# Six transfers with rows of 2 KB in place of two with rows of 8 and 4 KB for each expert's weights

## The reference, cut to what matters

```python
TOPK, E, h, i = 2, 16, 512, 256
probs = jax.nn.softmax(xt @ Wr.T + bias, axis=-1)
topk_val, topk_idx = jax.lax.top_k(probs, TOPK)
w = topk_val / (jnp.sum(topk_val, axis=-1, keepdims=True) + EPS)
g = jnp.einsum('th,ehi->tei', xt, Wg)
u = jnp.einsum('th,ehi->tei', xt, Wu)
y = jnp.einsum('tei,eih->teh', jax.nn.silu(g) * u, Wd)
routed = jnp.einsum('tke,tk,teh->th', one_hot(topk_idx), w, y)
shared = (jax.nn.silu(xt @ sWg) * (xt @ sWu)) @ sWd
```

## Time and profile before

| | |
|---|---|
| median of 3 runs | 1112.99 us (1108.66 to 1118.93) |
| the profiled execution | 1113.7 us, of which the span from the first to the last instruction is 1111.8 us |
| mean granted TensorE clock | 0.964 of full speed |
| PE busy over the span | 1005.3 us (90%) |
| POOL busy over the span | 298.5 us (27%) |
| DMA, mean over the span | 103 GB/s, 44573 packets |
| q1 (SyncE's), q0 (GpSimd's) | 26.7% and 11.9% of the 16 engines' span |

### The profile page before, as it was taken

One profiled execution on the slowest core, in us unless ns is written; L12 is line 12 of the kernel. 1 busy time (PEld: TensorE's weight loads), 2 busy tenths in 40 slices (PEclk: granted clock), 3 DMA queues, 4 the chain that ended last, 5 costly groups with the idle time before them and its releaser, 6 DMA issues.

```text
span 1111.8 us, 22306 instructions
## 1 busy us (share of the span) xinstructions
PE 1005.3 (90%) x6879; PEld 643.5 (58%) x6880; DVE 551.8 (50%) x1422; ACT 499.1 (45%) x1195; POOL 298.5 (27%) x319
## 2 busy tenths in 40 slices
PE   6767699999989999899998899899998999899994
PEld 3323458576765857567585687778643444344442
DVE  7985347465645756365666677678511111111110
ACT  7512277676747777576768622211122222122221
POOL 1087220111102010020202036342223443344442
PEclk9889899999989999899999999999999999999998
DMA  5032733240513324041335111611288447944443
GB/s 200 29 86 83 180 77 81 67 112 6 135 45 77 78 57 98 32 110 45 78 78 192 41 75 58 244 69 48 78 253 237 89 89 198 290 87 85 94 85 47
DMA packets 44573, 114.37 MB, mean 103 GB/s; under 512 B 9332, under 2 KB 11380, under 8 KB 42162
## 3 DMA queue, kind: packets, MB, share of 16 engines
q1 hardware_dynamic: 32146, 87.14, 26.7%
q0 software_dynamic: 12320, 25.90, 11.9%
HBM read 53.03 MB, written 25.17 MB: 70 GB/s over the span
## 4 chain that ended last, share of the span: by engine, by line
PE 67%; DMA 9%; DVE 8%; issue 8%; POOL 4%; ACT 2%; POOLq 0%; ACTq 0%; DVEq 0%
PE psum L512 10%; PE psum L1241 10%; PE psum L478 7%; DMA out<-y_sb,slot_out 7%; PE psum L525 7%; PE psum L499 7%; PE psum L483 5%; PE psum L1320 5%; PE psum L1185 4%; PE psum L1169 3%; PE psum L1262 2%; PE psum L528 1%; PE psum L501 1%; PE psum L1284 1%; DMA x_rows<-xn_scratch,slot_tok 1%
## 5 line engine op out<-in xcount | busy, mean ns | idle before, releaser
L635 DVE TENSOR_REDUCE nmax<-psum 128x1 f32<-128x128 f32 (+7 forms) x256 | 192.3, 754 | 79.4 <-PE psum L501 72.2
L594 ACT ACTIVATE probs<-psum,nmax 128x128 f32<-128x128 f32 (+7 forms) x256 | 190.7, 745 | 51.0 <-DVE nmax L635 45.7
L1241 PE MATMUL psum<-attnT,x_T 128*128 x376 | 180.9, 604 | 4.2 <-issue 2.4
L512 PE MATMUL psum<-ident,probs 128*128 128x128 f32 x1152 | 176.1, 279 | 3.9 <-DVE probsT L581 1.5
L499 PE MATMUL psum<-k_stack,q_stack 128*128 128x512 f32 (+2 forms) x384 | 158.2, 466 | 22.5 <-issue 14.3
L579 ACT COPY probsT<-psum 128x512 f32<-128x512 f32 (+3 forms) x256 | 129.1, 504 | 57.4 <-PE psum L512 45.6
L1142 DVE COPY x_T<-psum 128x512 f32<-128x512 f32 x47 | 32.5, 692 | 240.5 <-PE psum L1284 240.5
L478 PE MATMUL psum<-xnT,w_unit 128*128 128x512 f32 x256 | 132.6, 608 | 0.2 <-ACT full L453 0.2
L512 PEld LDWEIGHTS psum<-ident,probs 128*128 128x128 f32 x1152 | 125.6, 143 | 9.1 <-DVE probsT L581 3.8
L425 POOL CAST part_hi<-full 128x512 fp32r<-128x512 f32 x32 | 19.6, 612 | 376.6 <-ACT full L453 268.7
L842 POOL DMA_INDIRECT out<-y_sb,slot_out x47 | 74.5, 1586 | 166.5 <-DMA out<-y_sb,slot_out 74.3
(11 more groups left out here) (220 smaller groups left out, 1440.4 us busy)
## 6 DMA issues: line engine op xcount, KB each, us to landing
attnT<-in_wgu SPq DMA_DIRECT2D x16, 1024.0 KB, 5.2
q_stack<-part_hi SPq DMA_DIRECT2D x64, 128.0 KB, 2.4
q_stack<-part_lo SPq DMA_DIRECT2D x64, 128.0 KB, 2.4
k_stack<-part_hi SPq DMA_DIRECT2D x64, 128.0 KB, 2.4
k_stack<-part_lo SPq DMA_DIRECT2D x64, 128.0 KB, 2.6
w_dn<-in_wd SPq DMA_DIRECT2D x16, 512.0 KB, 6.1
out<-acc SPq DMA_DIRECT2D x17, 256.0 KB, 2.0
hot_all<-xn SPq DMA_DIRECT2D x4, 1024.0 KB, 8.5
```

Of the source, the lines that this page charges most:

```text
L512: mm = pe.transpose(bank(4 + m % 2)[:, (j - 4 * k) * P:(j - 4 * k + 1) * P], probs[n % PSLOTS][:, j * P:(j + 1) * P], ident[:, :])
L594: act.activation(probs[n % PSLOTS][:, 0:(i + 1) * P], bank(2 * (n % 2), 2)[:, 0:(i + 1) * P], ACT.Exp, bias=nmax[:, n % 4:n % 4 + 1], scal ...
L635: dve.tensor_reduce(nmax[:, n % 4:n % 4 + 1], bank(2 * (n % 2), 2)[:, 0:(i + 1) * P], AX.X, ALU.min).then_inc(s_M, 1)
L1241: mm = pe.matmul(bank(2 + p), lhs(k), rhs(k), start=(k == 0), stop=(k == KC - 1), skip_group_check=True)
```

## The change

`load` issues an expert's weights as six transfers instead of two, one for each block of 128 along the contraction: four of 128 x 512 values for gate and up, two of 128 x 512 for down. Each transfer is 256 KB with one row of 2 KB for each partition. Before, gate and up were one transfer of 1 MB whose partition rows are 8 KB, and down one of 512 KB with rows of 4 KB. In HBM the rows of one such transfer now lie 8 KB apart (gate and up) and 4 KB apart (down), since the layout of the arrays is unchanged. The number that `ready` waits for follows (six times 16 for each round of the ring instead of two times 16). The bytes moved, the slots, the places in the program and all other waits are the same.

```diff
             def load(e, s):
-                src_gu = a["wgu"][bass.ds(e, 1), :, :, :].rearrange("o p k n -> (o p) k n")
-                src_dn = a["wd"][bass.ds(e, 1), :, :, :].rearrange("o p k n -> (o p) k n")
-                sp.dma_start(w_gu[:, s, :, :], src_gu).then_inc(s_wl[s], 16)
-                sp.dma_start(w_dn[:, s, :, :], src_dn).then_inc(s_wl[s], 16)
+                for k in range(KC):
+                    sp.dma_start(w_gu[:, s, k, :], a["wgu"][bass.ds(e, 1), :, k, :].rearrange("o p n -> (o p) n")
+                                 ).then_inc(s_wl[s], 16)
+                for k in range(2):
+                    sp.dma_start(w_dn[:, s, k, :], a["wd"][bass.ds(e, 1), :, k, :].rearrange("o p n -> (o p) n")
+                                 ).then_inc(s_wl[s], 16)
 
             def ready(m, s):
 
-                sp.wait_ge(s_wl[s], 32 * (m + 1))
+                sp.wait_ge(s_wl[s], 16 * (KC + 2) * (m + 1))
                 sp.sem_inc(s_wr, 1)
```

## The result

The changed kernel takes **1134.1 us** (median of 4 runs, 1131.6 to 1137.6) against 1113.0 before (1108.7 to 1118.9): a ratio of 1.0188, with a 95% interval of 1.0134 to 1.0242. That is 21 us slower. The forecast was 1116 us with a range of 1105 to 1127, so the time lies outside it. The profiled execution took 1131.6 us with a span of 1129.6, 17.8 more than the span of before.

A forecast was written before the change was run, and what follows sets the result against it. The prediction took SyncE's load-loop period to bound the two routed stretches. Twelve loads at +0.25 us each gave +3.0 us, with issue, completion, HBM gaps and the first four loads at nothing: 1116 us, range 1105 to 1127.

The forecast's parts named there:

- the period of the load loop is what the stretches are made of: Routed stage, loads of experts 4 to 9 and 10 to 15: SyncE's load period of 7.64 and 7.75 us holds the adds.
- +0.24 us a load: DMA engines: an expert's 1.573 MB in 2 KB rows takes 3.93 us instead of 3.69; 0.25 taken.
- the issue costs nothing: SyncE's six issues, 0.54 us apart, stay hidden behind the load's bytes, with 0.9 us of cover.
- completion ... is in the 0.25: Six semaphore posts per load instead of two add nothing beyond the 0.25 us for bytes; upper bound +1.2 a load.
- rival B: Routed stretches: adds take turns with loads, load period grows to 10.5 us; about +11 us, 1124 us; chance 0.15.
- The fixed 2.0 us for each transfer: Skill's cost beside the bytes: four more transfers would add 8 us a load if paid serially; the prediction set it aside.
- Rival D: Weight loads: strided or small reads run slower, +1.2 us a load, 14.4 us over twelve loads, 1127 us; chance 0.13.
- C: Routed stretches: adds get in and loads hardly pay; at most -11.5 us, 1101.5 us, likelier 1107; chance 0.17.
- E: Weight loads: no effect, since 8 KB rows are cut up on the way anyway; 1113 us; shares 0.55 with the forecast.

The follow-up runs named there:

- six transfers by partitions: Against the changed kernel, the six 256 KB transfers are cut by partitions (four of 32, two of 64) with 8 and 4 KB rows; 1145.6 us, ratio 1.0290.

## Why the prediction was wrong

**The bound was read one step too far.** The step "the period of the load loop is what the stretches are made of" does not hold for the kernel before: freeing SyncE there gained nothing. With adds and gathers left out TensorE ran through the first stretch without a wait, at a load period of 7.30 us. The prediction's own sum pointed there: it had expert 15 ready 4.9 us before TensorE began its tiles. The step does hold for the changed kernel in its second stretch, where the chain is the load loop's, and freeing SyncE gives back 17 us in all. The row that I took for proof, six waits for landings against one for TensorE, shows that SyncE was busy waiting, not that anyone waited for it.

**The cost of a load was mis-sized more than tenfold.** The step "+0.24 us a load" was measured at 2.9 (7.70 to 10.60 in the mean of both stretches). The experiments part it:
- 0.5 us for 2 KB rows, with the number of transfers unchanged and the engines to themselves. The forecast had 0.25 for bytes through full engines; that was half in size, and only about 0.1 of the 0.5 is longer work of the engines.
- 0.9 us for six transfers, with their gaps in HBM. Here "the issue costs nothing" was right (0.52 us each, as forecast), and "completion ... is in the 0.25" failed. The stretch of twelve back-to-back 256 KB transfers at 395 to 405 GB/s was no stand-in: it reads without gaps and its transfers stood in a queue that was already deep, while a load of the ring begins on idle engines and moves 271 to 365 GB/s in its middle. Which of the two differences counts was not tried apart.
- 1.5 us beside adds and gathers: 8.58 to 10.60 is 2.0, where the kernel before pays 0.5. Two transfers with small rows pay 1.9 of the same kind (7.70 to 9.63), so small rows are enough for it. They are not the only way: six transfers by partitions pay 1.4 with large rows (10.25 to 11.63). So more, smaller transfers and smaller rows each make a load slower beside GpSimd's transfers, and the two don't add up. That the engines take up the adds sooner when the pieces are smaller fits the landings of the adds, but how they share their time was not traced.

**What that part is, was rival B.** Its mechanism came out: adds pass loads (0.8 and 4.7 us before their load's landing), and the load pays. Its sizes came out too, but in part by luck: a period of 10.5 us was worked out, 10.84 and 10.36 measured, and the second stretch was to cost 11.8 us more and cost 11.0. B put 2.95 us on a load, 0.25 for its own bytes and 2.7 for the adds and gathers let in. Measured were 1.4 and 1.5, an error on each side, and the two cancel. I gave it 0.15, because nothing in the rows showed an add overtaking a load. That was the wrong question. Loads in the routed stage of the kernel before came in large pieces only, so its rows could not show what small ones do. B's reckoning missed on one side: in the first stretch it had a gain of 1 us, and 5.6 were lost. Adds there also landed late (6.6 us in the median, up to 8.3), as did gathers, and TensorE waited 8.3 us for rows. The premise that the add lands after 5.3 us failed; the add can pass a load but doesn't run undisturbed.

The Trainium skill's rule (page "DMA: Bandwidth & Descriptors", section "Queues, rings and completion order"), by which the engines take turns between queues a packet at a time, agrees with adds that pass loads now. No run here shows how large a packet in this sense is (the packets that the profile counts are single rows): two transfers in small rows and six in large rows both grow beside adds. The fixed 2.0 us for each transfer that the prediction takes from the same page is given there for transfers that GpSimd issues; four more transfers of SyncE cost 0.9 us here, not 8.

**Rival D** named strided or small reads as slow, +1.2 us each load. The load did grow by 1.4 us with the engines to itself, so D's size was near. Its cause was not: without the gaps 14 of the 21 us remain, clear of noise, and of the 1.4 us the small rows account for 0.5. D had no term for adds that pass.

**Rivals C and E** fell: nothing was gained, the rows of 8 KB went as single packets, and small rows do something by themselves.

**The clock** was in no term. In the timeline of PE in the changed kernel, the first gate and up behind the 5.5 us wait for weights takes 3.78 us, and one behind a short wait 1.98. A down step of two tiles earlier takes 3.46 us once and 1.88 the next time. That is near twice the length, as at the lower level of 1.2 GHz:

```profile
961.90 3.46 PE L1322 MATMUL psum<-w_dn,gated_T 128*128 x4
969.29 1.88 PE L1322 MATMUL psum<-w_dn,gated_T 128*128 x4
...
983.81 3.78 PE L1243 MATMUL psum<-attnT,x_T 128*128 x4 [5.54 <-SPq L742]
```

Such steps come on top of the waits in the second stretch; I have not priced them apart.

**The chances.** Slower by over 1% had 0.16. They hung on whether a load would grow by a quarter of a microsecond or by more than one. The bound of D, +1.2, was taken from a row of another kind of transfer, with no reason that excluded more.

Open: why the engines serve a fresh load of six small transfers more slowly. Divided by the share, its middle runs at about 343 GB/s, against 372 for two transfers with small rows and 415 for two with large ones. I have the size, not the cause, and the gaps in HBM were not taken out of it.

## What to carry to other kernels

A loop that issues transfers, waits for their landing and then issues the next has a period of its own. Before you change its transfers, find out how much its period may grow before its consumers wait (here 0.8 us, an estimate by rival B's reckoning), and consider waiting one round later: that edit made six small transfers nearly as good as two large ones. Where a transfer shares the engines with another queue's, the number and the size of its pieces also bear on what it loses to the other queue, so a price read while it runs alone is too low (here 1.4 us alone, 2.9 in company). A wait on an engine proves a bound only if someone waits for that engine.

## What the runs showed of the hardware that I had not expected

- Six transfers of 256 KB, issued 0.52 us apart with nothing else in the queue, keep the DMA engines busy for about 5.0 us, two larger ones with 2 KB rows for 4.5, and two with 8 and 4 KB rows for 4.4. In single windows of 1 us they move at most 397, 416 and 438 GB/s.
- Transfers over 32 or 64 partitions with rows of 8 and 4 KB are slower than transfers of the same size over 128 partitions with rows of 2 KB: a load of six takes a period of 10.2 us against 8.6, with the engines to themselves. The engines are not idle in that time: in the third microsecond of a load the share is 1.13 in the mean, and they move 234 GB/s.
- A row of a weight load is one packet in the profile's count, whether of 2, 4 or 8 KB, and each transfer adds 16: q1 counts 32,146 packets before, 34,450 with three transfers, 40,338 with two in small rows and 41,362 with six.
- The accumulating scatters (128 rows of 2 KB for each tile) cost a load of six transfers in 2 KB rows 1.4 us of period, the gathers of the same size 0.7; a load in two transfers with 8 and 4 KB rows pays 0.3 and 0.2. These are differences of single executions.
